# Attention on TensorE: scores in runs of four tiles, the projections and the output product in one run, all sixteen blocks of value products in one run

## The reference

```python
q = (x @ W_Query + B_Query).reshape(B, Lq, 16, 64)      # x: (8, 512, 256), W: (256, 1024)
k = (ctx @ W_Key + B_Key).reshape(B, Lk, 16, 64)
v = (ctx @ W_Value + B_Value).reshape(B, Lk, 16, 64)
scores = einsum('bqhd,bkhd->bhqk', q, k) / 64 ** 0.5
probs = softmax(scores, axis=-1)
out = einsum('bhqk,bkhd->bqhd', probs, v).reshape(B, Lq, 1024)
x = x + out @ W_Output + B_Output
```

## Time and profile before

| | |
|---|---|
| Runs shown | 1678.03 us median of 3 (1676.47 to 1680.26) |
| Profiled execution, its own time | 1671.62 us |
| Its span, first to last instruction | 1669.9 us |
| Attention on TensorE, first projection to last output | 433.4 to 1476.9 us |
| TensorE matmul busy over the span | 1498.7 us (90%) |
| VectorE busy | 1121.9 us (67%) |
| ScalarE busy | 730.7 us (44%) |
| GpSimd busy | 601.9 us (36%) |

### The profile page before, as it was taken

How to read it: one execution, slowest core, us unless ns; L and a number is a source line. 1 busy time by engine, 2 the same in 40 slices (tenths; PEclk the granted TensorE clock), 3 DMA queues, 4 the chain that set the end, 5 groups by cost and what they waited for, 6 DMA issues and landing times. The chain is left out here.

```text
span 1669.9 us, 52044 instructions
## 1 busy us (share of the span) xinstructions
PE 1498.7 (90%) x22101; PEld 974.4 (58%) x22101; DVE 1121.9 (67%) x2625; ACT 730.7 (44%) x1678; POOL 601.9 (36%) x730
## 2 busy tenths in 40 slices
PE   6669999999699999999999999999999999943683
PEld 4457777776365655666656666665665666532452
DVE  7434556552477787787777777777787777757760
ACT  3324444442355555555455555555555555512120
POOL 2033444443233333333333333333333333310585
PEclk9659999999899999999999999999999999976797
DMA  7200000000533334333343433434334333431354
GB/s 236 74 13 13 13 14 13 1 1 0 151 76 90 87 82 106 81 91 95 93 96 86 103 81 94 108 74 103 84 91 98 96 91 81 107 114 20 66 84 56
DMA packets 94792, 127.92 MB, mean 77 GB/s; under 512 B 19552, under 2 KB 51552, under 8 KB 94560
## 3 DMA queue, kind: packets, MB, share of 16 engines
q1 hardware_dynamic: 88416, 116.07, 27.6%
q0 software_dynamic: 6144, 8.52, 3.2%
HBM read 94.95 MB, written 29.62 MB: 75 GB/s over the span
## 5 line engine op out<-in xcount | busy, mean ns | idle before, releaser
L1151 POOL TENSOR_SCALAR at_Pr<-at_Pr,at_rinv 128x512 f32<-128x512 f32 x512 | 350.0, 692 | 672.4 <-DVE at_rinv L1169 672.0
L1110 ACT ACTIVATE at_Pr<-at_ps,at_nmax 128x512 f32<-128x512 f32 x512 | 348.6, 685 | 321.9 <-DVE at_nmax L1162 321.9
L1176 DVE STREAM_TRANSPOSE at_blocks<-at_Pr 128x512 f32<-128x512 f32 x512 | 358.7, 701 | 62.7 <-POOL at_Pr L1151 62.6
L1162 DVE TENSOR_REDUCE at_nmax<-at_ps 128x1 f32<-128x512 f32 x512 | 325.2, 675 | 74.6 <-PE at_ps L983 74.6
L996 PEld LDWEIGHTS at_ps<-at_blocks,at_V 32*64 32x64 f32 x16384 | 239.1, 130 | 105.7 <-issue 62.3
L983 PE MATMUL at_ps<-at_k,at_q 64*128 64x512 f32 x1024 | 289.1, 641 | 6.9 <-ACT at_Pr L1110 6.1
L996 PE MATMUL at_ps<-at_blocks,at_V 32*64 32x128 f32 x16384 | 272.6, 274 | 6.7 <-issue 4.6
L983 PEld LDWEIGHTS at_ps<-at_k,at_q 64*128 64x128 f32 x1024 | 77.2, 185 | 126.9 <-ACT at_Pr L1110 64.1
L1169 DVE RECIPROCAL at_rinv<-at_rsum 128x1 f32<-128x1 f32 x512 | 72.5, 142 | 99.1 <-ACT at_Pr L1110 99.1
L1009 PE MATMUL at_ps<-at_wo,at_oT 128*128 128x256 f32 x512 | 121.3, 380 | 2.3 <-ACT at_oT L1092 2.3
L1009 PEld LDWEIGHTS at_ps<-at_wo,at_oT 128*128 128x128 f32 x512 | 97.2, 190 | 42.5 <-issue 29.1
(11 more groups left out here) (231 smaller groups left out, 1659.9 us busy)
## 6 DMA issues: line engine op xcount, KB each, us to landing
at_V<-spread_v SPq DMA_DIRECT2D x256, 256.0 KB, 4.7
spread_v<-at_V SPq DMA_DIRECT2D x64, 256.0 KB, 2.1
k_x<-in_x SPq DMA_DIRECT2D x8, 512.0 KB, 8.6
mg_ctx<-in_ctx SPq DMA_DIRECT2D x8, 512.0 KB, 9.3
mx_ctxn<-in_ctx SPq DMA_DIRECT2D x8, 512.0 KB, 3.6
rows<-m_ctxT SPq DMA_DIRECT2D x16, 256.0 KB, 5.8
out<-k_x SPq DMA_DIRECT2D x16, 256.0 KB, 5.2
r_w<-in_L_ffn_w SPq DMA_DIRECT2D x16, 256.0 KB, 5.7
```

The costliest lines, as they stand in the source:

```text
L1110: act.activation(Pr[:, n % P_RING, :], bank(n), ACT.Exp, bias=nmax[:, at], accum_out=rsum[:, at]).then_inc(s["exp"], 1)
L1151: pool.tensor_scalar(Pr[:, at, :], Pr[:, at, :], rinv[:, at:at + 1], 1.0, ALU.mult, ALU.mult).then_inc(s["pn"], 1)
L1162: dve.tensor_reduce(nmax[:, n % P_RING:n % P_RING + 1], bank(n), AX.X, ALU.max, negate=True).then_inc(s["nmax"], 1)
L1176: dve.transpose(blocks[:, u % 2, h, :, m, :], Pr[:, n % P_RING, :].rearrange("p (n q) -> p n q", n=KB)).then_inc(s["blocks"], 1)
```

## The change

TensorE's order becomes, for unit u: scores m = 0 and m = 1; output of unit u-2; q of unit u+1; k of unit u+1; the router's work, if any; V of unit u+1; scores m = 2 and m = 3; all sixteen blocks of the value products of unit u-1. The score ring has four banks, and q, k, V and the router's work use those four banks between the two groups of scores, each as soon as the exponential of the tile in it is done (`free`, `beside`). VectorE works in groups of four tiles: four maxima, then four times a reciprocal and a turned tile of the group before. ScalarE does four exponentials, q, k, the router's rows, V, and four exponentials. `Pr` has seven slots. V4 is filled by sixteen DMAs of 64 KB for a unit straight from V, with no copy in DRAM. A constant row of ones in the router gets a buffer of its own; there is no other edit outside of `attention`.

```diff
-    VALUES_AT = TILES - 2
-    S_RING, P_RING = 3, 6
+    S_RING, P_RING = 4, 7
+    Q_AT, K_AT, V_AT, ROWS_AT = 0, 1, 2, 3
...
-        def values_bank(u):
-            return bank(TILES * (u - 1) + VALUES_AT)
+        def beside(u, tile):
+            return bank(TILES * (u - 1) + tile)
...
                 def spread_values(u):
                     sp.wait_ge(s["V"], u + 1)
-                    wait_count(sp, s["V4"], 16 * QG * (u - 1))
-                    sp.dma_start(spread_v[u % 2], V[:, u % 2, :, :].rearrange("p t d -> p (t d)")
-                                 ).then_inc(s["v_out"], 16)
-                    sp.wait_ge(s["v_out"], 16 * (u + 1))
                     wait_count(sp, s["pv"], u - 1)
-                    for g in range(QG):
-                        sp.dma_start(V4[QW * g:QW * g + QW, u % 2, :, :, :].rearrange("p c t d -> p c (t d)"),
-                                     spread_v[u % 2].rearrange("(c r) f -> r c f", r=QW)).then_inc(s["V4"], 16)
+                    for n in range(QG):
+                        for g in range(QG):
+                            sp.dma_start(V4[QW * g:QW * g + QW, u % 2, n, :, :],
+                                         V[QW * n:QW * n + QW, u % 2, :, :]).then_inc(s[f"V4_{u % 2}"], 16)
...
+                def free(u, tile):
+                    wait_count(pe, s["exp"], TILES * (u - 1) + tile + 1)
...
                 def score(u, m):
                     n = TILES * u + 2 * m
-                    wait_count(pe, s["exp"], n - 1)
+                    wait_count(pe, s["exp"], n - 2)
...
+                    if m == 2:
+                        pe.wait_ge(s["q"], min(u + 2, U))
+                        pe.wait_ge(s["k"], min(u + 2, U))
+                    if m == 3:
                         pe.wait_ge(s["V"], min(u + 2, U))
...
                 for u in range(U + 2):
-                    for m in range(SLOTS):
-                        if there(u):
-                            score(u, m)
-                        if m == 0:
-                            if there(u + 1):
-                                project(u + 1, 0, 0)
-                            if there(u - 2):
-                                output(u - 2, 0)
-                                output(u - 2, 1)
-                            if there(u + 1):
-                                project(u + 1, 0, 1)
-                        if m == 1 and there(u - 1):
-                            weigh_values(u - 1, 0, KB // 2)
...
-                        if m == 2 and there(u + 1):
-                            project_values(u + 1)
-                            project(u + 1, 1, 0)
-                            project(u + 1, 1, 1)
-                        if m == 3 and there(u - 1):
-                            weigh_values(u - 1, KB // 2, KB)
...
+                    if there(u):
+                        score(u, 0)
+                        score(u, 1)
+                    if there(u - 2):
+                        output(u - 2)
+                    if there(u + 1):
+                        project(u + 1, 0)
+                        project(u + 1, 1)
...
+                        project_values(u + 1)
+                    if there(u):
+                        score(u, 2)
+                        score(u, 3)
+                    if there(u - 1):
+                        weigh_values(u - 1, 0, KB)
...
                 for u in range(U + 2):
...
+                    if there(u - 2):
+                        heads_out(u - 2)
+                    if there(u):
+                        for h in range(2 * 2):
+                            weights_of(u, h // 2, h % 2)
+                    if there(u + 1):
+                        queries(u + 1)
+                        keys(u + 1)
...
+                        values(u + 1)
+                    if there(u):
+                        for h in range(2 * 2):
+                            weights_of(u, 2 + h // 2, h % 2)
...
+                def group(u, half, behind, half_behind):
+                    for i in range(4):
                         if there(u):
...
+                            row_max(u, 2 * half + i // 2, i % 2)
+                    for i in range(4):
                         if there(u):
...
+                            row_sum(u, 2 * half + i // 2, i % 2)
+                        if there(behind):
+                            turn(behind, 2 * half_behind + i // 2, i % 2)
+
+                for u in range(U + 1):
+                    group(u, 0, u - 1, 1)
...
+                    if there(u - 2):
+                        add_out(u - 2, 0)
+                        add_out(u - 2, 1)
+                    group(u, 1, u, 0)
...
+                    if routed(u, APPLY) is not None:
+                        for t in range(TPB):
+                            apply(routed(u, APPLY), t)
```

More of the change, by code:

```diff
@@ L825, in _, with attention @@
                     step(b)
-def attention(nc, c, x_all, xnT_all, ctxT_all, first, Wq, Wk, Wv, Wo, gate_w, lg, rows, rows_in, out, landed,
-              spread_v):
+def attention(nc, c, x_all, xnT_all, ctxT_all, first, Wq, Wk, Wv, Wo, gate_w, lg, rows, rows_in, out, landed):
     U = HP * B
@@ L942, in _, with project @@
             def _(pe):
-                def project(u, of, d):
-                    src = xnT_all if of == 0 else ctxT_all
+                def free(u, tile):
+                    wait_count(pe, s["exp"], TILES * (u - 1) + tile + 1)
+                def project(u, of):
+                    src, at = ((xnT_all, Q_AT), (ctxT_all, K_AT))[of]
                     b, hp = u // HP, u % HP
-                    if d == 0 and of == 0:
-                        wait_count(pe, s["k"], u)
+                    free(u, at)
+                    if of == 0:
                         pe.wait_ge(s["scaled"], min(u + 1, 2))
[L949 to L959, removed]
+                    for d in range(DC):
+                        ins = pe.matmul(beside(u, at), weights(of, d, hp), src[:, d, b * S:b * S + S],
+                                        start=d == 0, stop=d == DC - 1)
+                    ins.then_inc(s[("q_ps", "k_ps")[of]], 1)
                 def project_values(u):
                     b, hp = u // HP, u % HP
-                    wait_count(pe, s["exp"], TILES * (u - 1) + VALUES_AT - S_RING + 1)
+                    free(u, V_AT)
                     for t in range(TPB):
                         for d in range(DC):
-                            ins = pe.matmul(values_bank(u)[:, P * t:P * t + P],
+                            ins = pe.matmul(beside(u, V_AT)[:, P * t:P * t + P],
                                             ctxT_all[:, d, b * S + P * t:b * S + P * t + P], weights(2, d, hp),
@@ L1028, in map_gates @@
                         for d in range(DC):
-                            ins = pe.matmul(ps[:, A_BANK, E * t:E * t + E],
+                            ins = pe.matmul(to[:, E * t:E * t + E],
                                             xnT_all[:, d, b * S + P * t:b * S + P * t + P], gT[:, d, :],
@@ L1032, in map_gates @@
                     ins.then_inc(s["l_ps"], 1)
[L1034 to L1036 removed]
+                project(0, 0)
+                project(0, 1)
                 project_values(0)
                 for u in range(U + 2):
[L1039 to L1065 removed]
@@ L1066, in _ @@
-                pe.wait_ge(s["k"], U)
+                    if there(u):
[6 more added lines that the diff above has]
+                        project(u + 1, 1)
+                        if any(routed(u, r) is not None for r in (TURN, TURN + 1, GATE)):
+                            free(u + 1, ROWS_AT)
+                        for d in range(DC):
+                            if routed(u, TURN + d) is not None:
+                                turn_rows(routed(u, TURN + d), d, beside(u + 1, ROWS_AT))
+                        if routed(u, GATE) is not None:
+                            map_gates(routed(u, GATE), beside(u + 1, ROWS_AT))
+                        project_values(u + 1)
@@ L1245, in _ @@
+                for half in range(2):
+                    add_out(U - 1, half)
+                    take_stats(LAST, 2 * half)
+                    take_stats(LAST, 2 * half + 1)
                 finish_stats(LAST)
@@ L1665, in _, with build @@
                         read(e + AHEAD)
-def build(nc, a, rows, out, spread_v):
+def build(nc, a, rows, out):
     with ExitStack() as ctx:
@@ L1678, in build @@
         lg = sb("lg", [P, NT, E], F32)
-        setup(nc, c)
         with ExitStack() as mid:
@@ L1745 @@
     out = nc.dram_tensor("out_0", (N + SPARE, D), F32, kind="ExternalOutput").ap()
-    spread_v = nc.dram_tensor("spread_v", (2, P, S), F32, kind="Internal").ap()
-    build(nc, aps, rows, out, spread_v)
+    build(nc, aps, rows, out)
     r = run(nc, [arrays], core_ids=[0])
```

133 lines of the change are left out of this document (54 added, 79 removed).

## The result

The changed kernel takes 1733.16 us (median of 4 runs, 1726.34 to 1740.94) against 1677.86 us (4 runs, 1676.47 to 1680.26). The ratio is 1.0329, 95% interval 1.0284 to 1.0375: slower by 55 us. That lies inside the predicted range of 1680 to 1734, at its edge, and 27 us above the predicted 1706. So what is added up from the two traces must come to 69, and what is added up from medians to 55.

What follows compares the result with a forecast made beforehand. TensorE was taken to bound attention. Profiled 1671.6 us - 53 (joined stays) + 87 (starvation) - 5.4 (existing gaps) = 1700.2, and 6.4 up to the median gave 1706; range 1680 to 1734, held 8 times in 10.

Steps and rivals of the forecast that it cites:

- a stay has a price: TensorE in attention: each stay in one array form costs 0.20 us (scores, 128*128 work) or 0.25 (value products).
- 15.62 - 0.85: A TensorE unit in attention: 15.62 us before, less 0.85 saved by four stays instead of eight, about 53 us in all.
- A whole packet's worth inside the joined run starves TensorE: Joined value products: 512 instructions outrun packets of 254 that take 3.5 us to arrive; 87 us lost (63 to 110).
- Price: 1.38 us: Joined value products: TensorE's wait for instructions per unit, mean between 1.0 and 1.75, over 63 units 87 us.
- More is lost: Rival: no instruction lead at most limits (1730 us), or score seam keeps its price (1733), or clock falls; chance 0.12.
- The existing gaps: Value-product halves of the kernel before: 7 instruction gaps from 480 to 1440 us, 5.4 us, which go.
- What hides the rest: Attention's waits for ScalarE, VectorE and SyncE in the new order: they cost nothing, 0 to 14 us as the bound.
- `apply` and statistics: VectorE's extra work in attention: at most 14 units delayed by 1.0 us, 0 to 14 us.
- Head and tail: The first and last units of attention: counted as 0, with 3 us either way.
- V4's DMAs: SyncE's queue: sixteen issues take some 6.9 us a unit, wanted 27 us or more after starting; cost nothing.
- The forecast proper: Whole kernel: slower by 10 to 45 us, own range 1688 to 1724 us, chance 0.66.
- No starvation: Rival: instructions reach the joined value products in time, so the gain of 53 us stays; 1639 or 1625 us, chance 0.15.

Runs made afterwards that it cites:

- e1: The changed kernel with each value-product matmul serving both heads with the first head's weights, 256 instructions a run instead of 512: 1608.07 us, ratio 0.9583.
- e2: The kernel before with the same wide value products, second head's weights left out of the product: 1659.35 us, ratio 0.9889.
- e3: The changed kernel with the output's eight passes of 256 columns repeated in the middle of each unit's value products: 1753.55 us, ratio 1.0450.
- e6: The changed kernel with value products in halves again, and VectorE turning the unit's first four tiles ahead of the second group's maxima: 1644.24 us, ratio 0.9798.
- e8: The changed kernel with each unit's value products made twice in a row, a run of 1024 instructions: 2203.57 us, ratio 1.3129.
- e9: The changed kernel's TensorE order, with VectorE turning the unit's first four tiles ahead of the second maxima: 1726.11 us, ratio 1.0278.
- e7: The changed kernel with V4 filled through DRAM as before, one write and four reads of 256 KB a unit: 1723.86 us, ratio 1.0273.

## Why the prediction was right, point by point

- **TensorE bounds, and a stay has a price.** Right. The unit without its holes is 14.77 us, the 15.62 - 0.85 of the sum; e1 against e2 gives 51.3 us for the 53 predicted.
- **A whole packet's worth inside the joined run starves TensorE.** Right, and the cause is shown: with half the instructions in the same array time the gaps vanish (e1), with slow work between the halves all but some go (e3), with the halves apart they are as rare as before (e6), and with the run doubled TensorE is idle 4.4 us a unit for lack of instructions instead of 1.4 (e8).
- **Its size was too small.** The step was "Price: 1.38 us", one run's gap taken as the mean, and 63 to 110 us as its bounds. In the trace of the changed kernel the 56 runs of value products from 480 to 1440 take 315.7 us from start to start, 5.64 each and 1.85 more than 3.79: 116 us for 63 units, above the upper bound. Three things were missing. A hole costs its idle time and some 0.4 more: 1.48 for the 1.09 idle at 1018.50, where the prediction added 0.27. The supply of a packet's worth is 3.6 to 3.8 us, where I had read 3.5. And where the first limit falls before the middle of the run, both limits starve (1.29 and 1.66 idle at 808.76 and 812.51); I had put such second gaps down as small. That is so in 10 of the 56 units, which lose 3.1 us each; the other 46 lose 1.6.
- **The clock was left out of the sum.** It stands only in the rival "More is lost". The kernel before has a granted clock of 1.00 from 440 us to the end of attention. The changed one has 17 us of withheld clock there: seven falls of some 1.7 us each, and 5 us in a stretch of 10 us around 1536, among the last units. Together with a few holes behind the run this makes the scores and the output from 480 to 1440 take 12 us more than 1.92 and 1.83 each.
- **The existing gaps.** I priced them at 5.4. From start to start the halves of the kernel before take 8.0 us more than 2.02 each from 480 to 1440, in seven halves with an idle stretch and seven without one.
- **The sum mended.** From the traces: - 53 + 116 + 12 - 8 = +67 us, beside 69.3 between the profiled executions. From the medians: - 51 (e1, e2) + 114 (e3) + 2 (e3 keeps 10 and the kernel before 8) = +65 us, beside +55. The intervals of e1, e2 and e3 leave about 9 us, so some microseconds stay open here.
- **What hides the rest.** Right where it was seen: no wait for an exponential ahead of q or the second scores in the unit shown, VectorE's groups cost nothing beside starving (e9). The 0 to 14 us given to `apply` and statistics did not show: from 480 to 1440 q waits for an exponential once, for 0.2 us. Head and tail: what follows attention has the same length, but the slow clock among the last units is some 5 us that the 3 either way did not cover.
- **V4's DMAs.** No gap is put down to them; e7 leaves some 9 us open.
- **The forecast and the range.** The forecast proper, 10 to 45 us slower, was missed by 10. The range held because it was stretched over "More is lost", so the mechanism was foreseen and the number in part lucky. The low end of "1688 to 1724" does not follow from 1.0 us a unit either: 1678 - 53 - 5 + 63 is 1683.
- **The rivals.** "No starvation" is excluded by the trace of the changed kernel and by e8. "More is lost" came closer to the truth than the forecast: its 1730 rested on gaps near their full price, 1.75 a unit, which is what most of the excess was, and it named the clock. The Trainium skill, page "Runtime: NRT & Kernel Launch", section "Instruction fetch mechanics", gives TensorE room for 2048 instructions, filled in blocks of 256. The trace agrees with the block (808.76 to 812.51 is 256 instructions) and does not agree with the depth, by which a run of 512 or 1024 would not starve.

## What to carry to other kernels

Count instructions as well as array time. In these runs TensorE got 256 instructions in some 3.7 us; a stretch of small side-by-side matmuls that is denser than that and longer than one packet's worth was bound by its instruction supply, however ready its data were. Join runs of large matmuls (0.2 us was saved here for each stay in a form), but break dense runs with slow work, and before a piece is moved ask what wait it was covering.

## What was not expected of the hardware

The granted clock fell to its lower level in the middle of a kernel whose TensorE is busy 91% of that stretch: at 1036 after pauses of 1.09 and 1.71 us within 17 us, while the one pause of 1.31 in the kernel before and its six smaller ones left the clock of the whole stretch at 1.00. The pauses alone do not tell when it falls. Two and three units later TensorE pauses 1.31 and 1.72 us (at 1069.60 and 1086.12) within 18 us, and the clock from 1065 to 1101 stays at 1.00; in the 56 units from 480 to 1440, 54 of them with a pause of 0.3 to 1.9 us, it fell six times. What sets these six apart, no run here shows. The four runs of the changed kernel go with it: 1740.94 us at a mean clock of 0.942, 1733.75 at 0.946, 1732.58 at 0.947, 1726.34 at 0.948. They spread over 14.6 us, the four of the kernel before over 3.8; whether starving makes the time less even is not shown by so few.
